# Writing the second lookup's keys to memory by tile in a graph layer on one Trainium2 core

## The chip, the cores and the metric

The kernel runs on one core of one Trainium2 chip. The metric is the device time of one execution in microseconds (us). Steps of the kernel below are told by the engines' names: PE is TensorE, DVE is VectorE, ACT is ScalarE, POOL is GpSimd, SP is SyncE; PEld is PE's weight load.

## The reference, cut to what matters

`x` has 12500 nodes with 32 features, and there are 400000 edges sorted by `dst`.

```
msg = relu(x[src] + edge_attr)                     # [400000, 32]
agg = segment_sum(msg, dst, 12500)                 # [12500, 32]
y   = x + ((1 + eps) * x + agg) @ W.T + b
out = layernorm(y)                                 # over the 32 features
```

All is float32. The expensive part is `x[src]`, 400000 rows of 128 bytes, and the sum by `dst`.

## The kernel before, in words

A batch is 2048 edges, 16 tiles of 128 (line 21); there are 195 full batches and a short first one of 5 tiles, 196 in all. Of each full batch, 8 tiles get their rows of `x` by indirect DMA that POOL issues, one instruction per tile (lines 540 to 562, 8 per batch, 1565 in all). The other 8 tiles get theirs by a lookup that PE does with 0/1 matrices (the "marks"), from a copy of `x` in SBUF split into three bf16 parts.

The lookup of a batch has two stages. In the first, DVE and ACT compare the `slots` of the batch, broadcast to all partitions, with each partition's number and give `oh1` (lines 759, 993 and 1000), and PE multiplies `oh1` by `xparts` (line 1154, 96 matmuls of 57 weight columns and 96 moving ones); ACT copies the result to `table` (line 968). In the second, the `keys` (one number for each of the 1024 looked-up edges) are compared with the partition's number, in four blocks b of 128 rows: DVE marks blocks 0 to 2 (line 771), ACT block 3 with a square and a relu (lines 1012 and 1018). The marks lie in `oh2`, and PE multiplies them with `table` (line 1173): for each block b, tile t and part n one matmul with 128 weight columns, the marks of the 128 edges of tile t, and 128 moving columns, so 4 x 8 x 3 = 96 in a step, each with its own weight load. DVE picks the right 32 of the 128 columns into `rows_all` (line 786).

In memory and in `keys` the 1024 keys stand by edge: key (p, t) of partition p and tile t at place p * 8 + t. The marks are stored with a gap, 8 in a run of 10 (`PITCH`), so the weights of tile t are every tenth element:

```
def key_marks(b):
    return oh2[:, b, :].rearrange("p (e t) -> p e t", t=PITCH)[:, :, 0:LOOK]
```

Then DVE adds the edges to the rows (line 802), ACT takes the relu (line 983), DVE marks the `dst` (line 805), PE sums by `dst` (line 1184, 32 matmuls) and DVE adds the sums to the nodes (line 829).

The keys take this way: DVE gives `key` (line 745), SP writes it to `key_dram` (line 483, 128 partitions of 16 bytes), SP waits at line 490 until it has landed and broadcasts it from there to all 128 partitions (line 491). Between the two SP issues the edge loads (lines 475, 476) and the write of the slots (line 489); behind them it issues the broadcast of the slots (line 497). SP does this for the batch that is two ahead; the slots are used one step later, the keys two.

The order is written out by hand: each engine has a `step` that is called for s from -3 to 197, most of it in a hardware loop. In step s, PE does line 1154 of batch s, line 1184 of batch s - 1, line 1173 of batch s for b = 0 and 1, the slots of batch s + 2 (line 1220), b = 2, the ranks of batch s + 3 (lines 1205 to 1211, weights that lie in one run), and b = 3. DVE's step is lines 831 to 857: marks b = 0 and 1, a wait for PE's last block of the batch before (line 778), four picks, the ranks, `add_rows` (line 802), keys, slots, mark b = 2, the two marks of line 759, and line 805. POOL gathers batch s + 3 in step s. `add_rows` waits until all 8 gathers of its batch have landed (line 800), and there are 4 buffers of rows: a gather of batch b waits until batch b - 4 is summed (line 551) and for two counts of PE (lines 553 and 557).

Of the kernel before, what the change touches and what calls it, by code (L numbers as in the profile page):

```python
# [7 lines left out]
P = 128  # L8
# [3 lines left out]
def gnn_kernel(nc, x, src, dst, edge, weight, bias, eps, out):  # L12
    F32, I32, BF16 = mybir.dt.float32, mybir.dt.int32, mybir.dt.bfloat16
    F16, U16 = mybir.dt.float16, mybir.dt.uint16
    ALU, ACT, AX = mybir.AluOpType, mybir.ActivationFunctionType, mybir.AxisListType
# [3 lines left out]
    LOOK = 8  # L19
# [19 lines left out]
    COLS = P * LOOK  # L39
    SIDE = P // D  # L40
    GROUPS = EVEN // 2
    KEYS = GROUPS // SIDE
    BLOCKS = (SUBS + 1) * EVEN
    FOUND = SIDE * D
# [1 line left out]
    DVE_SUBS = SUBS - 1  # L46
    DVE_KEYS = KEYS - 1
    EARLY_KEYS = 2

    PITCH = LOOK + 2  # L50

    WINDOW = 40

# [62 lines left out]
    key_dram = nc.dram_tensor("key_dram", [RING, COLS], F16, kind="Internal").ap()  # L116

    ctx = ExitStack()
    with ctx:
        def sb(name, shape, dt=F32):  # L120
            return ctx.enter_context(nc.sbuf_tensor(name, shape, dt))

        def ps(name, cols=512):
            return ctx.enter_context(nc.psum_tensor(name, [P, cols], F32))

        def sem(name):
            return ctx.enter_context(nc.semaphore(name))
# [6 lines left out]

        xparts = sb("xparts", [P, BLOCKS, PARTS, D], BF16)
        oh1_store = sb("oh1", [P, SUBS * EVEN * D * 2], BF16)
        oh2 = sb("oh2", [P, KEYS, P * PITCH], BF16)
        slots = sb("slots", [P, 2, SLOTS], F16)
        keys = sb("keys", [P, RING, COLS], F16)
        table = sb("table", [P, KEYS, PARTS * FOUND], BF16)  # L140
# [6 lines left out]
        key = sb("key", [P, 2, LOOK], F16)  # L147
# [22 lines left out]
        minus_lanes = sb("minus_lanes", [P, KEYS])  # L170
        lanes = sb("lanes", [P, KEYS])
# [23 lines left out]
        far = sb("far", [P, TILES])  # L195
# [7 lines left out]
        found = ps("found", 2 * 512)  # L203
# [51 lines left out]
        key_written = sem("key_written")  # L255
# [5 lines left out]
        keys_squared = sem("keys_squared")  # L261
# [3 lines left out]
        oh2_ready = sem("oh2_ready")  # L265
# [73 lines left out]
        def has(st, ahead, count):  # L339
            return st.inside or 0 <= st.s + ahead < count  # L340

        def slot_of(st, ahead, n):
            return (st.u + ahead) % n

        def uses(st, ahead):

            return st.turns + (st.u + ahead) // RING
# [10 lines left out]
        def wait_count(eng, semaphore, count):  # L358
            if not (isinstance(count, int) and count <= 0):
                eng.wait_ge(semaphore, count)  # L360
# [34 lines left out]
        aggX_v = aggX[0:SUMS, 0:NODES].rearrange("f (t p i) -> f i t p", p=NP, i=NEAR)  # L395

        def key_marks(b):
            return oh2[:, b, :].rearrange("p (e t) -> p e t", t=PITCH)[:, :, 0:LOOK]

        def by_edge(values):  # L400
            return values.rearrange("p (e t) -> p e t", t=LOOK)

        def turned_sources(k):

# [2 lines left out]
        def turned_late(k):  # L407

            tiles = range(LOOK)[k * LATE_TILES:(k + 1) * LATE_TILES]
            return tiles, found[:, k * 512:k * 512 + len(tiles) * (ROWS - P)].rearrange("p (t b) -> p t b", b=ROWS - P)  # L410
# [25 lines left out]
        def _(sp):  # L436
# [41 lines left out]
            def spread_keys(st):  # L478
                if has(st, 2, ROWS):
                    r, two, four = st.s + 2, slot_of(st, 2, 2), slot_of(st, 2, RING)  # L480

                    sp.wait_ge(key_ready, r + 1)
                    sp.dma_start(key_dram[four].rearrange("(p t) -> p t", t=LOOK), key[:, two, :]).then_inc(key_written, 16)

            def spread_slots(st):
                if has(st, 2, ROWS):
# [12 lines left out]
            def step(st):  # L499
                load_index(st)  # L500
                spread_keys(st)
                load_edges(st)
                spread_slots(st)
                if not st.inside and st.s == FROM + 2:

                    sp.wait_ge(nodes_ready, 2 * SPANS)
                    for p0, p1 in shares(NP):
                        sp.dma_start(x_sb[p0:p1, :, :], x_v[p0:p1, :, :]).then_inc(x_loaded, 16)
# [19 lines left out]
            for k, (t0, per) in enumerate(ROUNDS_OUT):  # L528
                t = slice(t0, t0 + per)
# [47 lines left out]
        def _(dve):  # L577
# [183 lines left out]
            def mark_keys(st, b):  # L761
                if has(st, 0, ROWS):
                    r, four = st.s, slot_of(st, 0, RING)
                    if b == 0:
                        if isinstance(r, int) and r == 0:

                            dve.wait_ge(sources_cast, 2)
                        dve.wait_ge(keys_loaded[four], uses(st, 0) * 16 + 16)

                    wait_count(dve, blocks_looked, (r - 1) * KEYS + (b + 1))  # L770
                    nc.vector.tensor_scalar(key_marks(b), by_edge(keys[:, four, :]), lanes[:, b:b + 1], None, ALU.is_equal).then_inc(oh2_ready, 1)  # L771

            def mark_sides(st):
                if has(st, -1, ROWS):
# [56 lines left out]
            def step(st):  # L831
                first, second = window_base(st, 0), window_base(st, 1)
                for b in range(EARLY_KEYS):
                    mark_keys(st, b)
# [18 lines left out]
                for b in range(EARLY_KEYS, DVE_KEYS):  # L853
                    mark_keys(st, b)
# [51 lines left out]
            for k in range(len(ROUNDS_OUT) + 1):  # L906
# [4 lines left out]
                if k >= 1:  # L911
                    t0, per = ROUNDS_OUT[k - 1]
                    t = slice(t0 * NEAR, (t0 + per) * NEAR)
# [8 lines left out]
        def _(act):  # L922
# [79 lines left out]
            def square_keys(st, b):  # L1002
                if has(st, 0, ROWS):
                    r, four = st.s, slot_of(st, 0, RING)
                    if b == DVE_KEYS:
                        if isinstance(r, int) and r == 0:

                            act.wait_ge(sources_cast, 2)
                        act.wait_ge(keys_loaded[four], uses(st, 0) * 16 + 16)

                    wait_count(act, blocks_looked, (r - 1) * KEYS + (b + 1))
                    nc.scalar.activation(key_marks(b), by_edge(keys[:, four, :]), ACT.Square, bias=minus_lanes[:, b:b + 1]).then_inc(keys_squared, 1)  # L1012

            def mark_keys(st):
                if has(st, 0, ROWS):
                    act.wait_ge(keys_squared, (st.s + 1) * (KEYS - DVE_KEYS))
                    at = key_marks(DVE_KEYS)
                    nc.scalar.activation(at, at, ACT.Relu, scale=-2.0, bias=1.0).then_inc(oh2_act_ready, 1)  # L1018

            def step(st):  # L1020
                if not st.inside and st.s == 0:
                    for k in range(1, TILES // 2, 2):
                        take_nodes(nc.scalar.copy, act, k)
                for b in range(DVE_KEYS, KEYS):
                    square_keys(st, b)
                for h in range(2):
                    fill_table(st, h)
                if not st.inside and st.s == 1:
                    turn_x()
                mark_keys(st)  # L1030
                relu(st)
                square_slots(st)
                copy_slots(st)
                mark_slots(st)
                if not st.inside and st.s == FROM + 1:
                    round_x(1, x_mid)
                if not st.inside and 0 <= st.s < 2:
                    clear_sums(st.s + 2)
# [16 lines left out]
            for k in range(rounds + 2):  # L1055
# [11 lines left out]
                if k >= 2:  # L1067
                    t0, per = ROUNDS_OUT[k - 2]
                    t = slice(t0 * NEAR, (t0 + per) * NEAR)
# [4 lines left out]
        def _(pe):  # L1074
# [11 lines left out]
            for k in range(2):  # L1086
                tiles, to = turned_late(k)
# [73 lines left out]
            def look_in_table(st, b):  # L1161
                if has(st, 0, ROWS):
                    r = st.s
                    if b == 0:
                        wait_count(pe, picked_ready, r * SIDE)
                    if b < DVE_KEYS:
                        pe.wait_ge(oh2_ready, r * DVE_KEYS + (b + 1))
                    else:
                        pe.wait_ge(oh2_act_ready, r + 1)
                    pe.wait_ge(table_ready, r * 2 + b * 2 // KEYS + 1)  # L1170
                    for t in range(LOOK):
                        for n in range(PARTS):
                            last = nc.tensor.matmul(  # L1173
                                found[:, t * FOUND:(t + 1) * FOUND], key_marks(b)[:, :, t],
                                table[:, b, n * FOUND:(n + 1) * FOUND],

                                start=(b == 0 and n == 0 and t % FOUND_BANK == 0), stop=(b == KEYS - 1 and n == PARTS - 1),
                                skip_group_check=True)
                    last.then_inc(blocks_looked, 1)
# [129 lines left out]
```

## Time and profile before

| | |
|---|---|
| time, median of 3 runs | 3029.05 us (3026.18 to 3032.44) |
| span of the profiled execution, first to last instruction | 2071.9 us |
| its own time | not given; the median less the span is 957.2 us |
| PE busy, granted clock | 97%, 0.993 |
| DVE, ACT, POOL busy | 80%, 76%, 73% |
| indirect DMAs | 1565 |
| DMA engines, mean busy share | 0.47 to 0.48 in the loop |

The profile is of one execution. "Busy" is the time in which an engine ran instructions; a row of the timeline gives start, duration, engine, line, operation and, in brackets, the idle time ahead of it with what ended it. Waits are put down to what came last. Semaphore and branch instructions don't count as busy.

### The profile page before, as it was taken

What the parts mean: (1) busy time and instruction counts of PE and PEld (TensorE: products, weight loads), DVE (VectorE), ACT (ScalarE), POOL (GpSimd) and SP (SyncE); (2) the same over time, 40 slices, a digit from 0 to 9 for tenths busy, and PEclk for the clock granted to TensorE, in tenths of its full rate; (3) what the DMA queues carried; (4) which work ended last, traced back from release to release, by engine and by line L of the source; (5) the groups of instructions that cost most, each with busy time, mean ns of one, the idle gap of its engine ahead of it and who ended that gap; (6) DMA issues with size and microseconds to landing.
All of it is one profiled execution on the core that took longest, in us unless ns stands there. A gap on an engine that the chain in (4) does not pass through costs nothing. (4 is left out here: it accounts for less than half of the span.)

```text
span 2071.9 us, 117127 instructions
## 1 busy us (share of the span) xinstructions
PE 2016.0 (97%) x46449; PEld 1922.5 (93%) x46449; DVE 1648.3 (80%) x4231; ACT 1565.9 (76%) x1616; POOL 1519.9 (73%) x1571
## 2 busy tenths in 40 slices
PE   4899999999999999999999999999999999999997
PEld 3899999999999999999999999999999999999994
DVE  7888778888888778888888877888888887788875
ACT  5777777777777777777777777777777777777773
POOL 6577777777777777777777777777777777777770
PEclk9999999999999999999999999999999999999998
DMA  6344454444444444544444444444444444444441
GB/s 163 84 111 113 113 114 114 112 110 109 110 111 112 112 113 114 114 110 110 110 110 110 114 112 113 112 114 109 110 110 110 111 113 113 111 114 114 110 110 34
DMA packets 236283, 228.68 MB, mean 110 GB/s; under 512 B 104218, under 2 KB 185556, under 8 KB 236062
## 3 DMA queue, kind: packets, MB, share of 16 engines
q1 hardware_dynamic: 186177, 202.59, 33.4%
q0 software_dynamic: 50080, 25.74, 13.3%
q8 instruction: 17, 0.28, 0.1%
q14 instruction: 9, 0.07, 0.0%
HBM read 225.43 MB, written 2.71 MB: 110 GB/s over the span
## 5 line engine op out<-in xcount | busy, mean ns | idle before, releaser
L541 POOL DMA_INDIRECT rows_all<-in_x,index x1565 | 1519.4, 971 | 502.8 <-issue 476.5
L1173 PE MATMUL found<-table,oh 128*128 128x128 bf16 x18720 | 1241.3, 225 | 11.5 <-issue 2.5
L1173 PEld LDWEIGHTS found<-table,oh 128*128 128x128 bf16 x18720 | 1168.1, 144 | 43.6 <-issue 20.0
L1012 ACT ACTIVATE oh<-keys,minus_lanes 128x1024 bf16<-128x1024 f16 x195 | 224.2, 1150 | 307.3 <-PE found L1173 294.5
L1154 PE MATMUL l<-xparts,oh 128*57 128x96 bf16 x18720 | 436.2, 207 | 0.9 <-ACT oh L1000 0.9
L1154 PEld LDWEIGHTS l<-xparts,oh 128*57 128x57 bf16 x18720 | 409.4, 108 | 14.0 <-issue 1.1
L993 ACT ACTIVATE oh<-slots,minus_lanes 128x1824 bf16<-128x1824 f16 x195 | 351.3, 1801 | 7.1 <-DMA slots<-slot_dram 7.1
L786 DVE COPY_PREDICATED rows_all<-mask,found 128x256 f32<-128x256 uint16 x780 | 343.1, 440 | 7.6 <-issue 1.4
L968 ACT CAST table<-l 128x768 bf16<-128x768 f32 x390 | 310.9, 798 | 39.7 <-PE l L1154 24.7
L1000 ACT ACTIVATE oh<-oh 128x1824 bf16<-128x1824 bf16 x195 | 335.7, 1721 | 0.0
L780 DVE TENSOR_TENSOR mask<-iota,side 128x32 f16<-128x32 f16 x195 | 37.5, 192 | 303.1 <-PE found L1173 291.0
L771 DVE TENSOR_SCALAR oh<-keys,lanes 128x1024 bf16<-128x1024 f16 x585 | 274.5, 496 | 2.5 <-issue 1.4
L759 DVE TENSOR_SCALAR oh<-slots,lanes 128x1824 bf16<-128x1824 f16 x390 | 272.2, 739 | 1.7 <-DMA slots<-slot_dram 1.7
L1184 PE MATMUL win<-onehots,relus 128*32 128x40 f32 x6250 | 239.8, 204 | 7.0 <-DVE aggX L829 6.8
L1184 PEld LDWEIGHTS win<-onehots,relus 128*32 128x32 f32 x6250 | 216.0, 113 | 21.0 <-DVE aggX L829 7.1
L1018 ACT ACTIVATE oh<-oh 128x1024 bf16<-128x1024 bf16 x195 | 206.9, 1061 | 0.0
L983 ACT ACTIVATE relus<-msg 128x512 f32<-128x512 f32 (+1 forms) x196 | 123.8, 631 | 99.1 <-DVE msg L802 88.7
L805 DVE TENSOR_TENSOR onehots<-win,rel 128x640 f32<-128x640 f32 (+1 forms) x196 | 157.3, 803 | 0.5 <-PE win L1184 0.5
L802 DVE TENSOR_TENSOR msg<-rows_all,msg 128x512 f32<-128x512 f32 (+1 forms) x196 | 133.1, 679 | 0.1
L829 DVE TENSOR_TENSOR aggX<-aggX,win 32x40 f32 x391 | 73.2, 187 | 64.1 <-issue 8.0
L750 DVE TENSOR_TENSOR in_slot<-ranks,bucket 128x456 f16<-128x456 f32 x195 | 121.2, 621 | 0.0
L722 DVE TENSOR_TENSOR counts<-ob,ranks 128x256 f16<-128x256 f16 x195 | 82.1, 421 | 14.6 <-DVE rows_all L786 6.9
(126 smaller groups left out, 906.5 us busy)
## 6 DMA issues: line engine op xcount, KB each, us to landing
slots<-slot_dram SPq DMA_DIRECT2D x195, 456.0 KB
msg<-in_edge SPq DMA_DIRECT2D x390, 128.0 KB
keys<-key_dram SPq DMA_DIRECT2D x195, 256.0 KB
rows_all<-in_x,index POOLq DMA_INDIRECT x1565
index<-in_src SPq DMA_DIRECT2D x195, 4.0 KB
key_dram<-key SPq DMA_DIRECT2D x195, 2.0 KB
slot_dram<-slot_row SPq DMA_DIRECT2D x195, 3.6 KB
oh<-in_x SPq DMA_DIRECT2D x3, 512.0 KB, 6.2
```

Source lines behind the costliest of these rows:

```text
L541: pool.indirect_dma_start(to, None, x, bass.IndirectOffsetOnAxis(indices[:, j:j + 1], 0)).then_inc(done, 16)
L759: nc.vector.tensor_scalar(oh1[:, j, :], slots[:, two, :], lanes[:, j:j + 1], None, ALU.is_equal).then_inc(oh1_ready, 1)
L771: nc.vector.tensor_scalar(key_marks(b), by_edge(keys[:, four, :]), lanes[:, b:b + 1], None, ALU.is_equal).then_inc(oh2_ready, 1)
L786: nc.vector.copy_predicated(rows[slot][:, POOLED * D:ROW].rearrange("p (t f) -> p t f", f=D), mask[:, two, :, k:k + 1].bitcast(U16).to_bro ...
L968: nc.scalar.copy(table[:, some, :], l1_all[:, :].rearrange("p (k c) -> p k c", k=KEYS)[:, some, 0:PARTS * FOUND]).then_inc(table_ready, 1)
L993: nc.scalar.activation(oh1[:, DVE_SUBS, :], slots[:, two, :], ACT.Square, bias=minus_lanes[:, DVE_SUBS:DVE_SUBS + 1]).then_inc(slots_squar ...
L1000: nc.scalar.activation(at, at, ACT.Relu, scale=-2.0, bias=1.0).then_inc(oh1_act_ready, 1)
L1012: nc.scalar.activation(key_marks(b), by_edge(keys[:, four, :]), ACT.Square, bias=minus_lanes[:, b:b + 1]).then_inc(keys_squared, 1)
L1018: nc.scalar.activation(at, at, ACT.Relu, scale=-2.0, bias=1.0).then_inc(oh2_act_ready, 1)
L1154: last = nc.tensor.matmul(l1_of(g)[half * HALF:half * HALF + CAP, :, :], oh1[:, j, b * CAP:(b + 1) * CAP], xparts[:, j * EVEN + b, :, :], ...
L1173: last = nc.tensor.matmul(found[:, t * FOUND:(t + 1) * FOUND], key_marks(b)[:, :, t], table[:, b, n * FOUND:(n + 1) * FOUND],  start=(b == ...
L1184: last = nc.tensor.matmul(win_sums(g), relus[:, j, :], onehots[:, j, :], start=(j == tiles.start), stop=(j == tiles.stop - 1))
```

## The change

Keys go to `key_dram` by tile, key (p, t) at place t * 128 + p. The broadcast is unchanged, so `keys` in SBUF stands by tile too; the marks are written in the same order without gaps, and the weights of a tile are 128 elements in one run. `oh2` shrinks from 1280 to 1024 elements per block. The DMA of line 483 is issued by the same engine at the same place, from the same 16 bytes per partition; each of its 1024 numbers of 2 bytes now has its own place in memory, 256 bytes from the next one of its partition.

```
-    PITCH = LOOK + 2
...
-        oh2 = sb("oh2", [P, KEYS, P * PITCH], BF16)
+        oh2 = sb("oh2", [P, KEYS, COLS], BF16)
...
         def key_marks(b):
-            return oh2[:, b, :].rearrange("p (e t) -> p e t", t=PITCH)[:, :, 0:LOOK]
-
-        def by_edge(values):
-            return values.rearrange("p (e t) -> p e t", t=LOOK)
+            return oh2[:, b, :]
+
+        def tile_marks(b, t):
+            return oh2[:, b, t * P:(t + 1) * P]
...
-                    sp.dma_start(key_dram[four].rearrange("(p t) -> p t", t=LOOK), key[:, two, :]).then_inc(key_written, 16)
+                    with nc.allow_non_contiguous_dma(reason="keys go to memory by tile, a partition's eight far apart"):
+                        sp.dma_start(key_dram[four].rearrange("(t p) -> p t", t=LOOK), key[:, two, :]).then_inc(key_written, 16)
...
-                    nc.vector.tensor_scalar(key_marks(b), by_edge(keys[:, four, :]), lanes[:, b:b + 1], None, ALU.is_equal).then_inc(oh2_ready, 1)
+                    nc.vector.tensor_scalar(key_marks(b), keys[:, four, :], lanes[:, b:b + 1], None, ALU.is_equal).then_inc(oh2_ready, 1)
...
-                    nc.scalar.activation(key_marks(b), by_edge(keys[:, four, :]), ACT.Square, bias=minus_lanes[:, b:b + 1]).then_inc(keys_squared, 1)
+                    nc.scalar.activation(key_marks(b), keys[:, four, :], ACT.Square, bias=minus_lanes[:, b:b + 1]).then_inc(keys_squared, 1)
...
-                                found[:, t * FOUND:(t + 1) * FOUND], key_marks(b)[:, :, t],
+                                found[:, t * FOUND:(t + 1) * FOUND], tile_marks(b, t),
```

## Rows read from the trace of the kernel before

**Rows 1.** The page: span, and PE's busy time with its share.
```profile
span 2071.9 us, 117127 instructions
...
PE 2016.0 (97%) x46449; PEld 1922.5 (93%) x46449; DVE 1648.3 (80%) x4231; ACT 1565.9 (76%) x1616; POOL 1519.9 (73%) x1571
```
**Rows 2.** Timeline of PE, one step: start us, duration us, engine, line.
```profile
1003.31 3.03 PE L1173 MATMUL found<-table,oh 128*128 128x128 bf16 x48
1006.27 0.41 PE L1220 MATMUL ranks<-in_slot,placed 128*32 128x57 f16 x8
1006.61 1.67 PE L1173 MATMUL found<-table,oh 128*128 128x128 bf16 x24
1008.12 0.27 PE L1205 MATMUL ranks<-ob,before 128*128 128x256 f16 x1
...
1008.45 1.61 PE L1173 MATMUL found<-table,oh 128*128 128x128 bf16 x24
1009.99 2.23 PE L1154 MATMUL l<-xparts,oh 128*57 128x96 bf16 x96
```
**Rows 3.** Waits: engine, line, waited for, us in total, times, longest.
```profile
DVE mask L780 <- PE found L1173: 291.0, 184, 2.7
```
**Rows 4.** Groups by shape, weight loads: busy us, mean ns, idle before.
```profile
L1173 PEld LDWEIGHTS found<-table,oh 128*128 128x128 bf16 x18720 | 1168.1, 144 | 43.6 <-issue 20.0 <-ACT x_turned L959 0.5 <-DVE rows_all L786 0.2
...
L1207 PEld LDWEIGHTS ranks<-ob,ones 128*128 128x128 f16 x195 | 19.1, 98 | 0.0
```
**Rows 5.** Line 541, durations ns min/median/max, first and last start; then timeline of POOL.
```profile
L541 POOL DMA_INDIRECT rows_all<-in_x,index x1565: 940/944/4226, 11.9 to 2022.3; - x196
...
1004.51 0.94 POOL L541 DMA_INDIRECT rows_all<-in_x,index  x1 [0.30 <-issue]
1005.76 0.94 POOL L541 DMA_INDIRECT rows_all<-in_x,index  x1 [0.30 <-issue]
```
**Rows 6.** Timeline, gathers that last longer and DVE instructions beside them.
```profile
113.01 1.28 DVE L759 TENSOR_SCALAR oh<-slots,lanes 128x1824 bf16<-128x1824 f16 x2
113.14 1.36 POOL L541 DMA_INDIRECT rows_all<-in_x,index  x1 [0.30 <-issue]
...
1003.17 1.04 POOL L541 DMA_INDIRECT rows_all<-in_x,index  x1 [0.30 <-issue]
...
1003.64 0.68 DVE L802 TENSOR_TENSOR msg<-rows_all,msg 128x512 f32<-128x512 f32 x1
...
1198.86 1.46 POOL L541 DMA_INDIRECT rows_all<-in_x,index  x1 [0.31 <-issue]
```
**Rows 7.** Windows: busy us (instructions) of PE, PEld, DVE, ACT, POOL; clock; DMA.
```profile
96.57:198.42 101.85, 101.04 (x2373) 97.24 (x2371) 81.92 (x210) 78.27 (x80) 77.65 (x79) 1.00 0.48 112
```
**Rows 8.** Windows of line 541 alone: POOL busy us (instructions), clock, DMA.
```profile
198.42:2012.08 1813.66, 1378.49 (x1428) 1.00 0.47 112
```
**Rows 9.** Timeline, the last gather of batch 194 and its user.
```profile
2012.08 1.13 POOL L541 DMA_INDIRECT rows_all<-in_x,index  x1 [0.30 <-issue]
...
2026.75 0.69 DVE L802 TENSOR_TENSOR msg<-rows_all,msg 128x512 f32<-128x512 f32 x1
```
**Rows 10.** SP: a wait (as in rows 3), its queue on the page, the timeline.
```profile
SPq L491 <- DMA key_dram<-key: 2.8, 9, 0.6
...
q1 hardware_dynamic: 186177, 202.59, 33.4%
...
999.23 0.32 SPq L497 DMA_DIRECT2D slots<-slot_dram  x1
...
1004.43 0.32 SPq L483 DMA_DIRECT2D key_dram<-key  x1
...
1004.89 1.80 ACT L993 ACTIVATE oh<-slots,minus_lanes 128x1824 bf16<-128x1824 f16 x1
...
1007.38 0.36 SPq L491 DMA_DIRECT2D keys<-key_dram  x1
```
**Rows 11.** Line 771, durations ns min/median/max, first and last start.
```profile
L771 DVE TENSOR_SCALAR oh<-keys,lanes x585: 470/482/712, 45.0 to 2027.4; 128x1024 bf16<-128x1024 f16 x195
```

## The prediction

> **What bounds the kernel now.** I read the page first: PE is busy for 97% of a span of 2071.9 us [rows 1]. The waits come next: DVE stands in each step until PE has done its last block, 291.0 us over 184 waits, 1.6 us in a step [rows 3], and in the loop PE itself hardly stands still, 101.04 busy of 101.85 us [rows 7]. So PE sets the pace: the next step's line 1154 follows the last block at once [rows 2], and a step takes about 10.1 us.
>
> But POOL is as full, which its 73% hides. A gather lasts 0.94 us and 0.30 us of issue follow, so one starts every 1.25 us [rows 5]; 8 of them make 10.0 us, only 0.15 under the step. The 0.30 isn't counted as busy. Between 198.42 and 2012.08 us, 1428 gathers start in 1813.66 us, 1.270 each, 10.16 per 8 [rows 8]. Some last longer than 0.94: 1.36 and 1.46 beside the pair of DVE marks of line 759, and 1.04 where line 802 runs [rows 6]. What POOL has to spare is a lead: the last gather of batch 194 starts at 2012.08, is over at 2013.21, and is used at 2026.75 [rows 9], 13.5 us later.
>
> **The change on PE.** The 96 matmuls of line 1173 run in three lots: 1003.31 to 1006.27, 1006.61 to 1008.12 and 1008.45 to 1009.99 [rows 2], 6.01 us, 63 ns each. Between two of these lots, from 1008.12 to 1008.45, stand the five matmuls of lines 1205 to 1211, whose weights lie in runs: 256 + 128 + 192 + 128 + 64 = 768 moving columns in 0.33 us, 0.43 ns a column, so 55 ns for 128. Their weight load takes 98 ns, that of line 1173 144 ns [rows 4], with the same 128 columns and 2 bytes; what differs is the step of 10 elements. The change removes that step. 96 x (63 - 55) = 0.7 us less in a step. From below the gain is nothing, if the 63 ns have another cause; from above it is these 0.7 us, since no row has 128 columns faster. I take 0.7, the nearest row being the same load in the same step. For 195 steps that would be 137 us, were PE alone.
>
> The Trainium skill, TensorE: Matmul & The Clock Gate, section Weight-path perf modes, speaks against that: it lets the fast weight load work on packed or strided columns alike, with column steps up to 1,024 elements. The trace disagrees, 144 against 98 ns; by the page the change would bring nothing on PE, and the sum would be zero instead of what follows.
>
> **What is late next.** A PE step of 9.4 us is under POOL's 10.0, so POOL's lead is eaten at over half a us in a step and gone after some 20 to 30 steps. From then on line 802 waits for gathers, DVE's marks behind it wait with it, and PE waits for these. The sum is therefore POOL's. I count from 198.42 us, where POOL is already at its own pace and so gains nothing from a faster PE, to batch 194: 198.42 + 1428 x p for the start of its last gather, 0.94 for it, 1.5 for its landing (no row shows that; it lies between 0 and the 13.5 us of rows 9, and the small write of line 483 mostly lands within 2.95 us [rows 10], so I take half of that), then line 802, and behind it the same 2071.9 - 2026.75 = 45.15 us as now.
>
> All hangs on p, the time from gather to gather. From below it is 1.25, no gather held up. From above, one of 1.46 and one of 1.36 in each step instead of 0.94 would make (10.0 + 0.94) / 8 = 1.37. Before, POOL sits where it meets DVE least: PE's pace is slower than POOL's, so each step pushes it against line 802 once, for 0.1 us, and the other seven gathers fall between DVE's long instructions. Without the lead that place is lost: line 802 then follows the landing of the last gather, and lines 750, 771, 759 (twice) and 805 run back to back right after it, beside gathers 2 to 5 of the next batch. The nearest row for POOL away from its resting place is the stretch from 96.57 to 198.42 us, before it had settled: 79 gathers in 101.85 us [rows 7], 1.289 each, with gathers of 1.36 in it [rows 6]. I take 1.289. Then the last gather of batch 194 starts at 198.42 + 1840.7 = 2039.1, line 802 at 2041.6, and the end is 2086.7: 15 us more than the span of 2071.9. p = 1.2787 would be no change.
>
> The Trainium skill, SBUF — State Buffer, states in its section on engine ports that a POOL-issued DMA can't write its descriptors while a DVE instruction holds the port pair they share. The rows agree as far as they go (1.46 and 1.36 against 0.94), and if that lock is what holds the gathers, no layout of the marks takes it away.
>
> **The rest of the change.** DVE's three marks take 0.48 us each [rows 11] and ACT's square and relu read and write as many elements as before; with the gaps gone I cost them at nothing, within 0.1 us each either way, and 0.3 us in a step hides behind DVE's 1.6 us wait for PE, later behind its wait for gathers. If that cover went too, 0.3 us would be on the path.
> The write of the keys becomes 1024 pieces of 2 bytes instead of 128 of 16. Now it is issued at 1004.43, and the wait at line 490 ahead of the issue at 1007.38 cost 2.8 us in 9 of 195 steps, so it lands within 2.95 us. SP's queue has 186177 packets of 1.1 KB on average in 33.4% of 16 engines' span [rows 10], 59 ns each. At that price from above, 64 pieces per engine instead of 8 add 3.3 us to the landing, and 175,000 pieces 0.31 to the engines' share of 0.48; from below they add nothing. The nearest row to so small a piece is line 483's own, far below 59 ns in 2.95 us with all overheads, so I take 0.5 us. Behind the wait on SP stand the broadcasts of keys and slots. The slots go out at 999.23 and are first used at 1004.89, 5.66 us later, the keys a step later still. A landing of 3.5 us holds SP up by 0.5 us ahead of the keys' broadcast, and the slots' one, at 1009.3 in this step, isn't reached before a landing of 4.5 us; no path is touched.
>
> **Sum.** The profiled execution's own time isn't given; the median of 3029.05 is 957.2 us over its span, and I leave that part alone: 3029.05 + 15 = 3044.
>
> **The rivals.**
> A, POOL sets the pace and is rarely held up. p near 1.25 gives 2071.9 - 41 = 2031, so 2988; p = 1.265 gives 3010. For it: 1.25 is what most gathers show, and a place with few collisions may exist behind a landing too. Against it: the stretch of rows 7. It decides from p under 1.2787.
> B, the weights' step isn't what costs. PE keeps its pace, 3029. For it: the page's rule and that line 1173 also switches tiles; against it: 55 and 63 ns lie side by side in one step.
> C, the keys land late. From 4.5 us on SP's wait puts off the slots' broadcast, and at the latest from 10 us, when the 5.66 us are gone, the marks that need it; the broadcast's own time lies in those 5.66 us, so I take 7, more than twice the landing now. Each us beyond is a us in each step at most: a landing of 8 us costs up to 195 us, 3224. For it: eight times the pieces, each smaller; against it: the bound of 3.3 us more above.
>
> **How the numbers follow.** About 0.2%, 6 us, is what a measurement of this kernel can tell from no change; that is p between 1.2745 and 1.283. My forecast, POOL's pace with collisions, has 0.48: 0.36 slower, 0.09 the same, 0.03 faster. Rival A 0.34: 0.30 faster, 0.04 the same. Rival B 0.10: 0.07 the same, the rest even. Rival C 0.08, slower. Together faster 0.345, same 0.20, slower 0.455. Sure of little here, I let the range go from A's floor, 2988, to p = 1.32, one long gather and a half in each step: 198.42 + 1885 + 2.44 + 45.15 = 2131, 59 more, 3088; it leaves out most of C and the far ends. The forecast's own range is 3030 to 3088.
>
> **What the profile of after would show.** PE: a weight load of line 1173 near 98 ns, its lots at 55 ns a matmul, PE busy down to some 90% with waits of a us in each step for DVE. DVE: its wait at line 780 shorter, and a new one at line 802 for rows_all. POOL: still 0.30 of issue between gathers, no waits for PE, and a mean per gather that tells the case: 1.25 to 1.27 is A, 1.28 to 1.32 the forecast. Wrong in B's way: the load stays at 144 ns. In C's: SP waits at line 491 for several us and lines 993 and 759 for slots.

## The result and the profile after

| | before | after |
|---|---|---|
| median | 3027.61 us (4 runs, 3026.16 to 3032.44) | 4533.15 us (4 runs, 4496.74 to 4540.59) |
| profiled execution: time, span | span 2071.9 us | 4540.59 us, span 4538.3 us |
| PE busy, granted clock | 97%, 0.993 | 60%, 0.777 |

The ratio is 1.4951, with a 95% interval of 1.4915 to 1.4987: half as long again, where 3044 us was forecast. The time of a run lies only 2.3 us over its span here. So the 957 us between before's median and before's span were no part outside the span, as the prediction took them; the experiments settle where they belong.

The page of after, in the order of [rows 1] and [rows 10]: span, busy time, granted clock in tenths, the two DMA queues (packets, MB, share of 16 engines' span).

```profile
span 4538.3 us, 117127 instructions
PE 2721.4 (60%) x46449; PEld 2359.1 (52%) x46449; DVE 1658.6 (37%) x4231; ACT 1552.0 (34%) x1616; POOL 1533.4 (34%) x1571
PEclk9877877777787777777777877777878777777778
q0 software_dynamic: 50080, 25.74, 26.1%
q1 hardware_dynamic: 360897, 202.59, 23.5%
```

DVE and POOL were busy as long as in [rows 1], ACT a little less, PE 705 us longer, and all of them stand for most of the time. The bytes are the same; q1 has 174,720 packets more, which is 195 batches times the 896 pieces that each write of keys gained. The queue to look at first is q0, POOL's gathers, which the change doesn't touch: 50080 packets took 26.1% of 4538.3 us on 16 engines, 378 ns each, where the same kernel before shows 89 ns (13.4% of 2073.1 us, from a second page of before, shown with the experiments).

Groups of after: busy us, mean ns, idle time ahead and what ended it. Behind them the waits of after, as in [rows 3]: us in total, times, longest.

```profile
L1172 PE MATMUL found<-table,oh 128*128 128x128 bf16 x18720 | 1508.1, 242 | 861.9 <-issue 856.5
L1153 PE MATMUL l<-xparts,oh 128*57 128x96 bf16 x18720 | 766.1, 244 | 541.5 <-issue 538.6
L1172 PEld LDWEIGHTS found<-table,oh 128*128 128x128 bf16 x18720 | 1283.8, 109 | 987.8 <-issue 960.7
```
```profile
POOL rows_all L540 <- PE found L1172: 1268.5, 254, 15.4
DVE mask L779 <- PE found L1172: 1187.6, 127, 19.8
SPq L488 <- ACT slot_row L974: 1391.1, 161, 19.2
SPq L490 <- DMA key_dram<-key: 207.8, 27, 12.1
```

The weight load did fall, from 144 ns [rows 4] to 109. But PE stands for 1403 us ahead of its two large groups, nearly all of it put down to "issue": it waited for nothing that the profile shows. POOL and DVE wait for PE most of all. The 207.8 us of SP's wait for the keys to land are too low: the view counts a wait only where the landing that ended it is on record, and many landings aren't. The issue times show more. Nothing but the wait for the keys stands between the write of the slots (line 488) and the broadcast of the keys (line 490); in before 0.1 us of idle time lies between them, 26 us in all, and here 963 us, with over 1.5 us in 122 of 195 steps.

A step on the timeline of after (start us, duration us, engine, line, idle time ahead), to be read beside [rows 2, 10]:

```profile
2007.87 0.37 SPq L482 DMA_DIRECT2D key_dram<-key  x1
...
2013.94 0.33 SPq L488 DMA_DIRECT2D slot_dram<-slot_row  x1
...
2015.29 0.28 PE L1172 MATMUL found<-table,oh 128*128 128x128 bf16 x2
...
2016.88 0.94 POOL L540 DMA_INDIRECT rows_all<-in_x,index  x1 [0.30 <-issue]
2021.00 0.27 PE L1172 MATMUL found<-table,oh 128*128 128x128 bf16 x1 [5.44 <-issue]
...
2022.45 0.33 SPq L490 DMA_DIRECT2D keys<-key_dram  x1
...
2023.46 0.32 SPq L496 DMA_DIRECT2D slots<-slot_dram  x1
```

The keys' write is issued at 2007.87, and the broadcast behind it goes out at 2022.45, 14.6 us later; before, the two issues lay 2.95 us apart [rows 10]. The first 6.1 of these us SP waits for the slots to write, the rest for the keys to land. In those 14.6 us PE stops in the middle of a block whose inputs are all there, goes on matmul by matmul from 2021.00, and runs in lots again only behind 2025.

The DMA engines are not what takes so long. Packets of the queues between 2008.75 and 2009.25 us:

```profile
q1 hardware_dynamic: 771, 0.00, 68.3%
```

In this half microsecond 771 pieces leave, in 0.683 x 0.5 us x 16 engines, 7 ns each, and the trace has all 1024 started by 2009.44. The landing comes 13 us behind the last of them.

### The profile page after: what moved, and what is told of

Its sections match the earlier page's. It is cut to its first block and busy times, and to the rows that moved or that the text cites. A ratio compares the mean times of both kernels' runs of the same rounds, so it can differ in the third digit from the quotient of the medians.

```text
span 4538.3 us, 117127 instructions
## 1 busy us (share of the span) xinstructions
PE 2721.4 (60%) x46449; PEld 2359.1 (52%) x46449; DVE 1658.6 (37%) x4231; ACT 1552.0 (34%) x1616; POOL 1533.4 (34%) x1571
## 3 DMA queue, kind: packets, MB, share of 16 engines
q0 software_dynamic: 50080, 25.74, 26.1%
## 5 line engine op out<-in xcount | busy, mean ns | idle before, releaser
L1172 PE MATMUL found<-table,oh 128*128 128x128 bf16 x18720 | 1508.1, 242 | 861.9 <-issue 856.5
L1172 PEld LDWEIGHTS found<-table,oh 128*128 128x128 bf16 x18720 | 1283.8, 109 | 987.8 <-issue 960.7
L1153 PE MATMUL l<-xparts,oh 128*57 128x96 bf16 x18720 | 766.1, 244 | 541.5 <-issue 538.6
L1153 PEld LDWEIGHTS l<-xparts,oh 128*57 128x57 bf16 x18720 | 638.7, 135 | 670.2 <-issue 656.9
L974 ACT CAST slot_row<-ranks 32x57 f16<-32x57 f32 x195 | 38.3, 196 | 1062.1 <-remote 795.2
L1183 PE MATMUL win<-onehots,relus 128*32 128x40 f32 x6250 | 294.8, 224 | 14.2 <-issue 10.0
L1183 PEld LDWEIGHTS win<-onehots,relus 128*32 128x32 f32 x6250 | 268.0, 130 | 36.0 <-issue 15.3
L1204 PE MATMUL ranks<-ob,before 128*128 128x256 f16 x195 | 64.8, 333 | 291.2 <-ACT slot_row L974 193.1
L1204 PEld LDWEIGHTS ranks<-ob,before 128*128 128x128 f16 x195 | 21.2, 109 | 307.5 <-issue 306.0
L1219 PE MATMUL ranks<-in_slot,placed 128*32 128x57 f16 x1560 | 102.3, 200 | 82.7 <-issue 78.8
```

What stands on the lines that cost most here:

```text
L1153: last = nc.tensor.matmul(l1_of(g)[half * HALF:half * HALF + CAP, :, :], oh1[:, j, b * CAP:(b + 1) * CAP], xparts[:, j * EVEN + b, :, :], ...
L1172: last = nc.tensor.matmul(found[:, t * FOUND:(t + 1) * FOUND], tile_marks(b, t), table[:, b, n * FOUND:(n + 1) * FOUND],  start=(b == 0 an ...
L1183: last = nc.tensor.matmul(win_sums(g), relus[:, j, :], onehots[:, j, :], start=(j == tiles.start), stop=(j == tiles.stop - 1))
```

## The experiments

Theory when they began: the 1024 pieces of a write are what costs, wherever the matmuls and marks stand. Its rivals: the marks' new layout costs it, or the time between span and median. Differences in us are between medians on the same chip. Two kinds of chips turned up: on some, which I call quick, before takes 2075 to 2078 us, on others, called slow, 3028 to 3089; each run names its kind.

**Before, unchanged.** Edit: none.

> The kernel before, unchanged, profiled again, because the median of its runs (3029 us) and the span of its trace (2072 us) lie 957 us apart while the changed kernel's time and span lie 2 us apart. Theory A (the part outside the span is real and fixed): span again near 2072 and time near 3029. Theory B (the kernel runs in a slower way in the timed executions, held up in the loop, and the trace that was given shows a quicker execution): span within a few us of the time, near 3029, with PE standing for issue.

Measured, quick chip: 2077.57 us, ratio 1.0003 (0.9994 to 1.0013), span 2074.6 us. The time is the span and 2 to 3 us. So the given trace (span 2071.9) must be that of a quick chip and the given median that of a slow one.

**The change itself on a quick chip.**

> The changed kernel itself, beside the kernel before on the same chip, because the chip of the first comparison ran the kernel before in 3028 us and this one ran it in 2077. Theory N (its time is the load of the pieces and hardly the chip): near e3_extra_scatter's 4424 us, so 2.1 times before. Theory O (the ratio of 1.50 carries over): near 3110.

Measured: 4168.77 us beside 2075.25, ratio 2.0105 (2.0046 to 2.0164). Its page:

```profile
span 4169.1 us, 117127 instructions
...
PE 2627.9 (63%) x46449; PEld 2364.8 (57%) x46449; DVE 1653.6 (40%) x4231; ACT 1569.3 (38%) x1616; POOL 1519.9 (36%) x1571
...
q0 software_dynamic: 50080, 25.74, 36.2%
q1 hardware_dynamic: 360897, 202.59, 32.7%
```

On this kind of chip the change doubles the time: 2093.5 us more, 10.7 us in each of 195 steps. This is the pair to compare, since the given trace of before is of a quick chip and that of after isn't. The gathers' packets take 0.362 x 4169.1 x 16 / 50080 = 482 ns here, so the kind of chip isn't what lengthens them.

A round of SP on this chip, from one write of the keys to the next, and three waits:

```profile
2017.04 0.44 SPq L482 DMA_DIRECT2D key_dram<-key  x1
...
2024.15 0.33 SPq L488 DMA_DIRECT2D slot_dram<-slot_row  x1
2032.48 0.34 SPq L490 DMA_DIRECT2D keys<-key_dram  x1
2033.64 0.32 SPq L496 DMA_DIRECT2D slots<-slot_dram  x1
...
2034.64 0.43 SPq L482 DMA_DIRECT2D key_dram<-key  x1
```
```profile
DVE oh L758 <- DMA slots<-slot_dram: 1454.4, 183, 20.2
PE ranks L1204 <- ACT slot_row L974: 405.2, 128, 11.8
SPq L482 <- DVE key L744: 38.6, 30, 3.5
```

Here the round has no slack. In the mean of the steps 10 to 184, 18.5 us pass from the write of the keys to their broadcast, 1.3 to the slots' broadcast and 1.3 to the next write, together the 21.0 us of a step; in before the three are 3.0, 2.0 and 5.2 of 10.2 us. SP stands between lines 488 and 490 in every one of the 195 steps, 2093 us in all against 25 in before (that this equals the loss is chance), and hardly ever for a key to write, 38.6 us. The slots' broadcast is held up with the keys', and DVE and ACT wait for the slots, 1454.4 and 745.6 us. So by this trace the landing of the keys sets the pace on a quick chip; no run takes the wait away to confirm it. On the slow chip of the first comparison the round has slack: 16.1, 1.3 and 5.6 of 23.0 us, and SP waits 844.5 us for keys to write.

**Marks by tile, keys by edge.** The new layout of the marks without the new write: the marks read the keys with a step of 8.

```
-                    nc.vector.tensor_scalar(key_marks(b), by_edge(keys[:, four, :]), lanes[:, b:b + 1], None, ALU.is_equal).then_inc(oh2_ready, 1)
+                    nc.vector.tensor_scalar(key_marks_3(b), by_tile(keys[:, four, :]), lanes[:, b:b + 1], None, ALU.is_equal).then_inc(oh2_ready, 1)
```

> Keys stay by edge in memory and in SBUF, written in pieces of 16 bytes as before; only the marks are written by tile, read with a step of 8 elements. This is the layout part of the change alone. Theory 1 (the 2-byte pieces cost the 1500 us): no slower than before by more than 3%, line 1173's weight load near 98 ns, DVE's three marks up to 0.6 us longer each. Theory 2 (weights in runs make PE or its instruction supply stall): near 4500 us.

Measured, quick chip: 2388.33 us, ratio 1.1509 (1.1476 to 1.1542). Its groups (line 775 is before's 771, line 545 before's 541, line 1177 before's 1173):

```profile
L775 DVE TENSOR_SCALAR oh<-keys,lanes 128x1024 bf16<-128x1024 f16 x585 | 660.3, 1157 | 2.5 <-issue 1.4 <-PE found L1177 1.0
```
```profile
L545 POOL DMA_INDIRECT rows_all<-in_x,index x1565 | 1842.9, 1178 | 504.6 <-issue 455.6
L1177 PE MATMUL found<-table,oh 128*128 128x128 bf16 x18720 | 1184.9, 223 | 166.1 <-DVE oh L775 142.8
```

The layout of the marks alone loses 311 us, not 2093, and by another way: a mark that reads with a step takes 1157 ns in the mean instead of 496 (the median before is 482 [rows 11]), and POOL's gathers beside these marks grow from a mean of 972 to 1178 ns. PE's matmuls then wait for the marks, 142.8 us. Theory 1 had allowed 3% here: it had the longer marks, but not what they do to the gathers and to PE. The change itself doesn't read with a step, so these 311 us are the price of the detour and no part of the 2093. That leaves the write as their place.

**Before, and a second write of the keys in 1024 pieces.** Everything else is as before; the pieces go to spare memory that nobody reads.

```
+                    with nc.allow_non_contiguous_dma(reason="a second write, in pieces of two bytes"):
+                        sp.dma_start(key_spare[four].rearrange("(t p) -> p t", t=LOOK), key[:, two, :]).then_inc(spare_written, 16)
```

> The kernel before with a second write of the keys to a spare place, by tile in 2-byte pieces, whose landing only DVE's next but one key and the end wait for. This is the memory part of the change alone. Theory 1 (pieces): slower by 1000 us or more, near 4500, with PE standing for issue and gathers late. Theory 2 (layout): within 2% of before.

Measured, quick chip: 4424.45 us, ratio 2.1352 (2.1255 to 2.1448); 2347 us more, 12.0 in each step. Its waits and queues:

```profile
PEld l L1161 <- issue: 1047.7, 819, 10.6
SPq L502 <- DMA slot_dram<-slot_row: 1866.7, 180, 16.0
```
```profile
q1 hardware_dynamic: 388977, 203.00, 39.0%
q0 software_dynamic: 50080, 25.74, 24.7%
```

The write alone brings the whole loss and the same marks in the trace, PE's issue gaps and the gathers' longer packets. The write itself is waited for by DVE alone, before it fills the same buffer of keys again two steps later. But the slots' write stands behind it in SP's queue and lands late with it: SP waits 1866.7 us for that one, where before on the same kind of chip waits 296.0. From the second write to the slots' broadcast it is 20.0 us in the mean, of a step of 22.2. So this run shows that the pieces are the cause; it doesn't show that they cost anything apart from SP's round.

**Three ways to write the same bytes.** The second write once more: in 512 pieces of 4 bytes; in 1024 pieces of 2 bytes that lie 512 bytes apart in memory; and in 1024 pieces of 2 bytes into SBUF, 32 bytes apart.

```
-    key_spare = nc.dram_tensor("key_spare", [RING, COLS], F16, kind="Internal").ap()
+    key_spare = nc.dram_tensor("key_spare", [RING, COLS * 256], F16, kind="Internal").ap()
...
+                        sp.dma_start(key_spare[four].rearrange("(t p g) -> p t g", t=LOOK, p=P)[:, :, 0:1], key[:, two, :].rearrange("p (t g) -> p t g", g=1)).then_inc(spare_written, 16)
```

> The kernel before with a second write of the keys to a spare place in 512 pieces of 4 bytes instead of 1024 of 2. Theory N (a cost per piece): half of the 2347 us that 1024 pieces added, so near 3250. Theory L (pieces of many engines fall in the same line of memory and queue for it): as many sharers but half the writes, also 3250 or more. If under 2200, it is the 2-byte size.

> The kernel before with the second write in 1024 pieces of 2 bytes, each 512 bytes from the next place, so no two share a line. Theory L (shared lines): near before, under 2300. Theory N (a cost per piece, wherever it goes): near 4424.

> The kernel before with the second write in 1024 pieces of 2 bytes into SBUF, 32 bytes apart, nothing of it to memory. Theory N (a cost per piece in the DMA engines): near 4424. Theories L and M (small writes to memory are what costs): under 2300.

| second write, quick chips | time, us | ratio (95%) | more per step | per piece | landing |
|---|---|---|---|---|---|
| 1024 x 2 B side by side | 4424.45 | 2.1352 (2.1255 to 2.1448) | 12.0 us | 11.8 ns | 18.4 us |
| 512 x 4 B side by side | 3111.97 | 1.4953 (1.4904 to 1.5002) | 5.3 us | 10.4 ns | 10.0 us |
| 1024 x 2 B, 512 B apart | 2078.03 | 1.0011 (1.0001 to 1.0021) | 0.0 us | 0.0 ns | 4.1 us |
| 1024 x 2 B into SBUF | 2075.67 | 1.0001 (0.9991 to 1.0011) | 0.0 us | 0.0 ns | 3.9 us |

The landing is the time from the issue of the second write to the last landing of it that the trace recorded, the median of the steps. In the quick run of the change the keys' own write has 17.9 us, in before 1.4.

The queues of the kernel with pieces apart, and of before on the same kind of chip:

```profile
q1 hardware_dynamic: 388977, 203.00, 43.7%
q0 software_dynamic: 50080, 25.74, 17.1%
```
```profile
span 2073.1 us, 117127 instructions
...
PE 2018.5 (97%) x46449; PEld 1924.4 (93%) x46449; DVE 1650.0 (80%) x4231; ACT 1566.6 (76%) x1616; POOL 1521.3 (73%) x1571
...
q1 hardware_dynamic: 186177, 202.59, 33.0%
q0 software_dynamic: 50080, 25.74, 13.4%
```

So neither the number of pieces nor their size alone is the cost. The kernel with pieces apart has the same 388977 packets as the one that takes twice as long. Nor does a piece hold its DMA engine longer: summed by size from the packets of the traces, a 2-byte one took 8.6 ns in the mean side by side and 7.4 ns apart, and a 16-byte one of before 8.6. What grows is the landing, from 4.1 to 18.4 us, and the packets of others: those of the keys' broadcast (2048 bytes) take 441 ns instead of 106 in before, those of the gathers (1024 bytes) 648 instead of 169. What differs between the two runs is that all pieces of a write fall within 2 KB of memory. Whether it matters that they come from 16 engines wasn't tried, and the pieces into SBUF lie 32 bytes apart, so that run doesn't try neighbours there.

The loss per piece, 10.4 and 11.8 ns, is near the same for 512 and 1024 pieces, and the change's own, 2093.5 us over 195 x 1024, is 10.5. The landing grows by (18.4 - 4.1) / 1024 = 14 ns a piece, an estimate: as if the memory took neighbours one after another, long after the engines are rid of them. Before writes neighbours too, 128 pieces of 16 bytes in the same 2 KB, and they land in 1.4 us.

The Trainium skill, DMA: Bandwidth & Descriptors, section Specifications, gives 512 bytes as the least transfer for full rate and says that smaller ones are done as a read-modify-write. Pieces 512 bytes apart are as small, and cost at most 0.2%; the cost of small pieces here depends on where their neighbours go, which the section doesn't say. Its section Why small descriptors are slow excepts transfers from SBUF to SBUF. The run into SBUF agrees, 1.0001, but the run with pieces apart in memory does as well, 1.0011, so the two don't show the exception.

**The change's layout, keys turned on PE.** To have the weights in runs without the pieces: PE turns the keys with one matmul, ACT copies them out as 8 rows of 128, SP writes 8 runs of 256 bytes and broadcasts after the slots.

```
+                    sp.dma_start(key_dram[four].rearrange("(t p) -> t p", t=LOOK), key_row[:, two, :]).then_inc(key_written, 16)
...
+                    nc.scalar.copy(key_row[:, two, :], key_ps).then_inc(keys_copied, 1)
...
+                    nc.tensor.matmul(key_ps, key[:, slot_of(st, 2, 2), :], ident_half[:, :], start=True, stop=True)
```

> The layout of the change, but the keys are turned on PE (one matmul with the identity), copied by ACT and written as 8 runs of 256 bytes. Theory 1 (pieces): at or below the time before; with PE 0.7 us a step quicker POOL's gathers decide, so between 41 us less and 59 us more than before. Theory 2 (layout): near 4500 us.

Measured, quick chip: 2134.84 us, ratio 1.0277 (1.026 to 1.0295). Within PE's loop this version turns the same one of the two key buffers in every step, so it looks up other keys in one batch of two; the work is the same. The next version has one buffer of keys:

```
-                    nc.vector.tensor_tensor(key[:, slot_of(st, 2, 2), :], of_row(bucket, r), of_row(key_base, r), ALU.add).then_inc(key_ready, 1)
+                    nc.vector.tensor_tensor(key[:, 0, :], of_row(bucket, r), of_row(key_base, r), ALU.add).then_inc(key_ready, 1)
...
-                    nc.tensor.matmul(key_ps, key[:, slot_of(st, 2, 2), :], ident_half[:, :], start=True, stop=True)
+                    nc.tensor.matmul(key_ps, key[:, 0, :], ident_half[:, :], start=True, stop=True)
```

> e5_keys_turned with one buffer of the keys, so that the right keys are turned; nothing else is changed. Theory P (POOL's gathers, held up by DVE once their resting place is lost, set the pace): 2135 us as e5, 2.8% over before, gathers of 1.46 and 1.21 us in most steps, DVE waiting at line 796 for rows_all. Theory Q (e5 was slow for its wrong keys): at or under before.

> Layout of the change, keys turned on TensorE and written in runs of 256 bytes, as e7, on another chip. If the chip is one on which before takes about 2077 us (Theory P, the pace of a step passes to GpSimd's gathers, which VectorE holds up): about 2135 us, as e5, ratio 1.03, line of the messages on VectorE waiting for rows_all. If it is one on which before takes about 3050 us: ratio 0.99, as e7, with gaps of TensorE put down to issue.

Measured: on a slow chip 3066.17 us beside 3088.88, ratio 0.9927 (0.9914 to 0.994); on a quick one 2137.21 beside 2076.09, ratio 1.0297 (1.0283 to 1.0311). The layout that was wanted, without the pieces, is close to the prediction's own case; it has a matmul and a copy of ACT more in a step, and SP broadcasts the slots first. A step of it on the quick chip, DVE and POOL, with the window of line 536 (before's 541) behind it, as [rows 8]:

```profile
1015.87 0.69 DVE L796 TENSOR_TENSOR msg<-rows_all,msg 128x512 f32<-128x512 f32 x1 [0.83 <-DMA rows_all<-in_x,index]
1015.96 1.42 POOL L536 DMA_INDIRECT rows_all<-in_x,index  x1 [0.30 <-issue]
...
1016.89 0.62 DVE L744 TENSOR_TENSOR in_slot<-ranks,bucket 128x456 f16<-128x456 f32 x1
...
1017.68 1.21 POOL L536 DMA_INDIRECT rows_all<-in_x,index  x1 [0.30 <-PE found L1174]
...
1017.99 1.36 DVE L753 TENSOR_SCALAR oh<-slots,lanes 128x1824 bf16<-128x1824 f16 x2
...
1026.71 1.42 POOL L536 DMA_INDIRECT rows_all<-in_x,index  x1 [0.30 <-issue]
```
```profile
198.00:2000.00 1802.00, 1385.19 (x1368) 1.00 0.41 108
```
```profile
L1174 PEld LDWEIGHTS found<-table,oh x18720: 95/98/151, 46.8 to 2088.0; 128*128 128x128 bf16 x200
```

DVE's line 796 (before's 802) waits for rows. Right behind it come lines 744 and 753 (before's 750 and 759), and the gathers beside them last 1.42 and 1.21 us. From the long gather at 1015.96 to the next at 1026.71 it is 10.75 us, a step. Between 198 and 2000 us, about 173 steps, 159 gathers last over 1.3 us and 83 between 1.15 and 1.3, where before has 2 and 39. The gathers' packets take 56 ns each here (8.3% of 2128.5 us on 16 engines), against 89 in before; so even its 16-byte pieces may hold up others a little, which no run tries alone.

**The same, PE longer by 0.5 us.** The turn of the keys ten times instead of once in each step.

```
-                    nc.tensor.matmul(key_ps, key[:, 0, :], ident_half[:, :], start=True, stop=True)
+                    for again in range(10):
+                        nc.tensor.matmul(key_ps, key[:, 0, :], ident_half[:, :], start=True, stop=True)
```

> e7_keys_turned with the turn of the keys done ten times over, 9 x 56 ns = 0.5 us more of PE in each step and the same result. Theory P: PE is then just slower than POOL's 10.0 us a step again, POOL comes to rest against one DVE instruction, and the kernel gets quicker by doing more: 2040 to 2090 us, with few gathers over 1.1 us. Theory Q (PE or the longer way of the keys sets e7's pace): slower than e7 by up to 0.5 us x 195 = 98 us.

> e12 with nine more matmuls of the keys' turn in each step, about 0.5 us of TensorE. Theory P: on a quick chip GpSimd sets the pace and this is hidden in part, or even a gain, because a step that TensorE lengthens lets the gathers run ahead: 2090 to 2145 us, below e12 plus 20. The rival (TensorE still sets the pace of a step of e12): e12 plus 90 to 100 us, for 0.5 us in each of about 195 steps. On a slow chip: about 20 us above e12, as before.

Measured: on the slow chip 3088.54 us beside 3088.88, ratio 1.0000 (0.9991 to 1.0008), 22 us over the version with one turn. On the quick one 2131.67 us, ratio 1.0275 (1.026 to 1.029), where the version with one turn has 1.0297 (1.0283 to 1.0311). The window of the gathers on the quick chip, and PE's busy time on its page:

```profile
198.00:2000.00 1802.00, 1385.37 (x1366) 1.00 0.41 108
```
```profile
PE 2039.8 (96%) x48399; PEld 1927.4 (90%) x48399; DVE 1663.4 (78%) x4231; ACT 1583.2 (74%) x1811; POOL 1590.3 (74%) x1571
```

PE works 86 us more than in the version with one turn (2039.8 against 1953.6) and the time doesn't grow. PE isn't what the step waits for; POOL is, with 1366 and 1368 gathers in the same 1802 us: 1385.19 us of work and 1368 times 0.30 of issue fill 1796 of them. A gain by more work of PE, down to 2040 to 2090 us as the first of the two expectations had it, didn't come. The 22 us on the slow chip are a quarter of those 86, so there PE's own work isn't all of the pace either, and POOL couldn't be tested there.

**Before, for its profile.**

> The kernel before, unchanged, for its profile on this chip. The same time as before, ratio 1.00. If the chip is a slow one (about 3050 us): TensorE's idle time in the loop of the matmuls is put down to issue, several hundred microseconds of it, in steps without a single piece of keys; if these gaps are absent, the slow chips lose the time elsewhere. On a quick chip: nearly no issue time, as in the given profile.

The chip was a quick one: 2075.9 us, ratio 1.000 (0.999 to 1.001), PE's idle time ahead of its two large groups 11.3 and 0.9 us. A profile of before on a slow chip is not to be had from these runs. The nearest is the version with turned keys on the slow chip, PE only:

```profile
1009.54 0.20 PE L1155 MATMUL l<-xparts,oh 128*57 128x96 bf16 x1 [0.51 <-issue]
1010.25 1.85 PE L1155 MATMUL l<-xparts,oh 128*57 128x96 bf16 x76 [0.50 <-issue]
```
```profile
PE l L1155 <- issue: 494.9, 846, 1.9
PE found L1174 <- issue: 181.5, 403, 1.2
```

1249 gaps, most of half a microsecond, in a kernel without pieces. On the quick chip the same kernel stands for 9.1 us for issue ahead of line 1174 and for 0.8 us in all ahead of line 1155. It is the sign that after shows too, there with gaps up to 10.0 us. So part of the issue time of the first pair belongs to the slow chip and not to the change.

## Why the prediction was wrong, step by step

**The keys' write, the step that failed.** The prediction put it: "at that price from above, 64 pieces per engine instead of 8 add 3.3 us to the landing ... so I take 0.5 us". It so had a landing of 3.5 us. On a quick chip the last landing on record comes 17.9 us after the issue, and the broadcast follows the write by 18.5 us in the mean; on the slow one by 16.1. The price of a piece on its DMA engine was safe, 7.7 to 9.0 ns against the 59 taken, which was a mean over packets of all sizes. The mistake is that this price was taken to bound the landing: in the step of after shown the pieces have left within 0.7 us and land 13 us later, and that time is in no packet of the write. The one row of before with neighbours in memory, line 483's own 128 pieces of 16 bytes, landed within 2.95 us [rows 10], so no row could bound the landing from above, and the range should have been open upwards there.

**Its reach.** "No path is touched" rested on the 3.5 us and fell with them. Rival C had the cause, keys written in pieces, and on quick chips the path and the price too, and was given 0.08. It let the loss come by SP and the slots, one us a step for each us behind 7: 18.5 less 7 is 11.5 us, and 10.7 were measured. Its signs are there, SP at line 490 and lines 992 and 758 waiting for slots. What held it down was the bound of 3.3 us. Neither the forecast nor C had that others suffer who don't touch the keys: PE stands for issue, and POOL's gathers take 378 ns a packet (482 on the quick chip) instead of 89. On quick chips, 4169.1 us of span against 2073.1, PE is busy for 609 us more (2627.9 less 2018.5) and idle for the other 1487. Of all its idle time there about 1080 us are put down to issue and 405.2 to ACT's copy of the slots, which is C's path. How much the issue gaps and the slow gathers would cost if SP's round weren't the longer one isn't shown; a run in which nobody waits for the pieces or for a write behind them would tell. On the slow chip, where the round has slack, they seem to have a larger part; that wasn't tried. Part of the 609 is its clock: the granted clock of that run is 0.775, a mean over its two levels of 2.4 and 1.2 GHz, where PE that hardly stands still had 0.993.

**The frame of the sum.** "I leave that part alone" put 957 us outside the span. There are 2 to 3 us. The 957 belong to the steps of a slow chip, where PE has gaps of its own. The size was wrong without that; but the sum described steps of 10.1 us, and the runs that it was to be compared with had steps half as long again.

**What was right, seen without the pieces.** The weight load of line 1173 takes 98 ns with keys turned on PE, where it took 144 [rows 4]. The Trainium skill, TensorE: Matmul & The Clock Gate, section Weight-path perf modes, has no difference between packed and strided columns; the trace is against it. The gain on PE was sized too high: the matmuls of the second lookup are busy for 1149.4 us in place of 1245.4, 0.49 us a step for 0.7. "The sum is therefore POOL's" held: adding 0.5 us of PE changed nothing, and POOL is full. By the same count it was full in before, 1378.49 and 1428 x 0.30 us of 1814 [rows 8]. The time from gather to gather was 1802.00 / 1368 = 1.317 us, against 1.289 taken and 1.32 as the upper end. With 1.317 the prediction's own count gives 198.42 + 1880.7 + 2.44 + 45.15 = 2126.7 for the end, and the span of that run is 2128.5; this tests the frame of the count, not p, which is measured here. The place where POOL is held up was right too, at the lines behind `add_rows`, at 1.42 and 1.21 us in the step shown. What the Trainium skill, SBUF — State Buffer, section SBUF: two separate sides, says of the shared port pair agrees with both; the runs don't show the lock itself. In size the forecast of +15 us was too low even so: this version has +61 (2137.21 less 2076.09), just outside the +59 that were its far end.

**What the change would need.** No version was faster on both kinds of chips. Turning the keys on PE gains 0.7% where before takes 3089 us and loses 3% where it takes 2076.

**Left open.** That PE's "issue" gaps are instructions coming late from memory would fit all of the above, gaps during the pieces, hardly any with pieces apart, and longer packets of the gathers in the same runs. No row shows it: the queues that the page calls "instruction" have 26 packets in all in before and 27 in after, far fewer than gaps, so it is a guess. What makes a chip slow wasn't found, nor whether it is the chip itself or what else ran on it. Whether 2 KB is the size within which pieces hinder each other, or some smaller one, wasn't tried: the runs have 2 and 4 bytes at one end and 512 at the other.

## What to carry to other kernels

Before a write is cut into pieces, ask where the neighbours of a piece go: 1024 pieces of 2 bytes cost at most 0.2% 512 bytes apart and 2347 us over 195 steps side by side, so turn the data on the chip, here with one matmul, and write runs. What an engine pays for a packet doesn't bound when the write lands; where somebody waits for the landing, take a row that shows it, or leave the range open. Check a wait that the profile calls small against the issue times on both sides of it. When a DMA gets worse, look also at everybody else who uses the memory: here the queue of gathers and the engines' "issue" time. And a median far from the profiled span is a question to settle first; it may be another chip.

## What was not expected of the hardware

- Writes of 2 or 4 bytes side by side cost the path 10 to 12 ns each. They leave the DMA engines at 7 to 9 ns each, but 1024 of them land only 18 us after the issue and 512 after 10 us, in the median. In every run with them PE, which doesn't read them, stands for issue, for up to 10.0 us at a time (the longest wait of line 1172 for issue in after).
- The same kernel takes 2075 to 2078 us on three chips and 3028 to 3089 in two other comparisons, each within 0.5% run after run.
- The change loses less on the slow chip (1505 us) than on the quick one (2093). Part of the gaps seems to be paid there already; that wasn't tried.
- A DVE mark that reads 2-byte keys with a step of 8 elements took 1157 ns in the mean against 496, and with it POOL's gathers were 21% longer in the mean (1178 against 972 ns).
